# Reordered moves, later bias sums and a copied half row in a deformable convolution kernel

## The chip, the cores and the metric

The kernel runs on one core of a Trainium2 chip. The metric is the device time of one execution in microseconds (us), the median of several runs. The core has five engines with instruction streams of their own: PE (TensorE, matrix products), DVE (VectorE), ACT (ScalarE), POOL (GpSimd) and SP (SyncE, which here issues nearly all DMA transfers). They meet through semaphores; a wait holds everything behind it on its engine.

## The reference

The input x has 8 images of 32 channels and 128 x 128 pixels. Two residual layers follow each other:

```
x1  = x  + conv1(gn(x))          # depthwise 3x3, then three 32x32 channel mixes
out = x1 + conv2(deform(gn(x1)), w_conv) + b_conv

gn(v):      (v - mean) / sqrt(var + 1e-5), per image and channel
deform(v):  off = conv3x3(v, w_off)         # two offsets for each pixel and channel
            at each pixel, v sampled at (row + off[0], col + off[1]),
            clipped to the image, bilinear between the four neighbours
conv2:      3x3, 32 -> 32 channels, zero padding
```

The depthwise convolution and the three mixes are folded into one 3x3 convolution's weights in the setup.

## The kernel before

**Layout.** An image lies in SBUF as 128 partitions: four row phases times 32 channels, with 32 blocks of rows along the free axis. Each 3x3 convolution runs as matmuls over two such tiles, one shifted against the other by two rows: xa and xb for conv1, x1a and x1b for the offsets, mapa and mapb for conv2. The group norm is not applied to the data: its scale goes into the weights (`w1`, `wo`, `w2`, one scaled copy per image, made by DVE), and its mean goes into the padding and into a bias. That bias is a product of the summed weights with the mean: a small matmul (`mean_sum`, L677, "bias sum" below), which ACT then reads from PSUM. There are three of them for each image: b1 (conv1), bo (offsets), b2 (conv2).

**Stages of an image.** conv1 in eight groups of matmuls (jobs "x1"), each evicted by ACT into x1a; then eight offset chunks (L762, 24 matmuls each; counted from 0). Behind each chunk ACT (`offset_parts`), DVE (`deform`) and POOL select and blend neighbours out of x1_strips, which is x1 laid out by strips of rows, and write `mapped`. SP moves `mapped` to mapa in two halves (16 moves each, L456, once four and once eight chunks are mapped) and copies mapa to mapb (L469, L470). Then conv2 runs in eight groups (jobs "c2") and DVE adds them onto x1a, from where SP stores them.

**Order on TensorE.** TensorE runs the chunks of image i; behind each chunk stands a list of jobs (`jobs_behind`): conv1 groups of the next image and conv2 groups of the one before. Image 0's chunks also carry the first three conv1 groups of image 2, with its b1 sum behind chunk 4 (`FURTHER_BIAS`). All jobs share three PSUM banks in turn: a job waits until the third job before it has been evicted (`bank`). A conv1 group 0 waits for `x_pads`, the padding of xa and xb that ACT writes in `pad_x`. The offsets of a chunk wait until the chunk two before it has been used by DVE (`off_used`).

**Order on ACT.** Chunk by chunk, written out by hand (L1017 and on): `offset_parts`, pads of `mapped` at chunks 1 and 5, `pad_x` of the image after next at the chunk `FURTHER_BIAS`, evictions of conv1 groups, `sum_far`, bias evictions, the pads of x1. `clamp` writes the edges of x1_strips after their moves have landed.

**Order on SP.** One stream. For image i: second half of the x1b copy, first mapb copy, the second mapa half and second mapb copy of the image before; loads of the image after next; then x1b's first half and 32 moves x1a to x1_strips for the next image (`move_strips`, L375), and behind these the first mapa half of image i.

**The last image.** Its conv2 reads xa and xb in place of mapa and mapb, in two parts: three groups read the first half of each strip's rows, five the second. The left half of the second part's columns is mapped with the sixth chunk, the right half with the eighth. SP moves the left columns to xa (`move_left_columns`, L479), and copies whole rows from xa to xb (1 MB); ACT, POOL and DVE then copy the right columns out of `mapped` into both tiles (12, 10 and 10 copies, `end_row`). DVE's copies stand behind its third addition of that image (`COPY_END_BEFORE`).

A second path for offsets beyond one pixel stands at the end and isn't taken here.

Of the kernel before, what the change touches and what calls it, by code (L numbers as in the profile page):

```python
# [13 lines left out]
def deformable_preact_kernel(nc, x, dw_w, pw_w, att_w, glob_w, off_w, conv_w, conv_b, out):  # L14
# [8 lines left out]
    Q = C  # L23
# [37 lines left out]
    END_GROUPS = [1, 2, 3, 4, 5, 6, 7, 0]  # L61
    END_PARTS = [0, 0, 0, 1, 1, 1, 1, 1]
    COPY_END_BEFORE = 3
    END_SETUP = 1
    END_BIAS = 5
    CONV2_SETUP = 2
    NEXT_BIAS = [6] * NB
    FURTHER_BIAS = [4] + [NK - 1] * (NB - 1)

    def spread(i):  # L70
        return isinstance(i, int) and NB - 2 <= i < NB
# [20 lines left out]
    def jobs_behind(i, k):  # L92
        jobs = []
        if i + 1 < NB:
            jobs += [("x1", i + 1, m) for m in conv1_groups(i, k)]
            jobs += [("x1", i + 2, m) for m in further_groups(i, k)]
            jobs += [("bo", i + 1, 0)] if k == NEXT_BIAS[i] else []
        if i >= 1:
            jobs += [("b2", i - 1, 0)] if k == (CONV2_SETUP if i + 1 < NB else END_SETUP) else []
            jobs += [("c2", i - 1, m) for m in (LAST_CONV2 if i + 1 < NB else END_CONV2)[k]]  # L100
        if i + 1 == NB and k == END_BIAS:
            jobs += [("b2", i, 0)]
        if i + 2 < NB and k == FURTHER_BIAS[i]:
            jobs += [("b1", i + 2, 0)]
        return jobs

# [10 lines left out]
    with ctx:  # L117
# [6 lines left out]
        def sem(name):  # L124
            return ctx.enter_context(nc.semaphore(name))
# [121 lines left out]
        end_copied = [sem(f"end_rows_copied{n}") for n in range(2)]  # L247
# [81 lines left out]
        def end_row(q, t, o, shifted):  # L329
            p = Q * (2 * t + o)  # L330
            b = NJ * (2 * o + t) + 4
            if not shifted:
                to = xa[Q * q:Q * q + Q, b:b + 4, 1 + WQ:WP]
            elif q < 2:
                to = xb[Q * (q + 2):Q * (q + 3), b:b + 4, 1 + WQ:WP]
            else:
                to = xb[Q * (q - 2):Q * (q - 1), b + 1:b + 5, 1 + WQ:WP]
            return to, mapped[p:p + Q, q, 4:8, 1 + WQ:WP]

        def stored_count(part, images):  # L340

# [79 lines left out]
        def _(sp):  # L421
# [37 lines left out]
            def move_mapa(half):  # L459
                move_rows(mapa, 4 * half, 4, mapa_moved[half])  # L460
# [49 lines left out]
            for i in range(NB):  # L510
                prev, nxt, after = i >= 1, i + 1 < NB, i + 2 < NB
                if prev:

                    sp.wait_ge(off_done, NK * i)
                    copy_x1b(i % 3, 1)
                    sp.wait_ge(map_pads, i)
                    sp.wait_ge(mapa_moved[0], A_MOVES * DMA * i)
                    copy_mapb(0)
                if nxt and i >= 2:
                    sp.wait_ge(out_ready, 8 * (i - 1))  # L520
                    store(sp, i - 2, (i - 2) % 3, 1)
                if prev:
                    sp.wait_ge(mapped_ready, NK * i)
                    if i >= 2:
                        sp.wait_ge(conv2_done, 8 * (i - 1))
                    sp.wait_ge(mapped_pads, 2 * i)
                    move_mapa(1)
                    sp.wait_ge(mapa_moved[1], A_MOVES * DMA * i)
                    copy_mapb(1)
                if after and prev:  # L530
                    for half in range(2):

                        sp.wait_ge(conv1_done, 8 * (i + 1) + (5 if half == 0 else 8))
                        load_xb(i + 2, half, xb_loaded)
                if nxt:

                    sp.wait_ge(x1_pads, i + 2)
                    sp.wait_ge(off_done, NK * i + 4)
                    copy_x1b((i + 1) % 3, 0)
                    sp.wait_ge(mapped_ready, NK * i + 4)  # L540
                    for half in range(2):
                        move_strips(sp, i + 1, half)
                if not nxt:
                    if i >= 2:
                        sp.wait_ge(out_ready, 8 * (i - 1))
# [7 lines left out]
                    copy_rows(xb, xa, 0, 4, end_copied[0])  # L553
                    sp.wait_ge(mapped_pads, 2 * i + 2)
                    sp.wait_ge(mapped_ready, NK * i + 6)
                    move_left_columns(end_moved[1])
                    sp.wait_ge(end_moved[1], A_MOVES * DMA)
                    copy_rows(xb, xa, 4, 4, end_copied[1])
                    sp.wait_ge(out_ready, 8 * i)
                    for part in range(2):  # L560
                        store(sp, i - 1, (i - 1) % 3, part)
                    break
                sp.wait_ge(mapped_ready, NK * i + 4)
                if prev:
                    sp.wait_ge(conv2_done, 8 * (i - 1) + 4)
                else:
                    sp.wait_ge(s_setup["dve"], 6)
                sp.wait_ge(mapped_pads, 2 * i + 1)
                move_mapa(0)
# [52 lines left out]
        def _(pe):  # L622
# [105 lines left out]
            def end_conv2(m, ps):  # L728
                if END_PARTS[m] == 0:
                    pe.wait_ge(end_moved[0], A_MOVES * DMA)  # L730
                    pe.wait_ge(end_copied[0], B_MOVES * DMA)
                else:
                    pe.wait_ge(end_moved[1], A_MOVES * DMA)
                    pe.wait_ge(end_copied[1], B_MOVES * DMA)
                    for e in END_SHARES:
                        pe.wait_ge(end_rows[e], 1)
                conv_group(ps, w2[(NB - 1) % 2], xb, xa, END_GROUPS[m], first2_done, True).then_inc(conv2_done, 1)
# [76 lines left out]
        def _(act):  # L814
# [200 lines left out]
            for i in range(NB):  # L1015
                prev, nxt = i >= 1, i + 1 < NB
                for k in range(NK):  # L1017
# [17 lines left out]
                    if prev and k == (CONV2_SETUP if nxt else END_SETUP):  # L1035
                        conv2_bias(i - 1, (i - 1) % 2, bank("b2", i - 1, 0))
                    if not nxt and k == END_BIAS + 1:
# [8 lines left out]
                    if k == 2:  # L1046
                        if not prev:
                            clamp(i, 1)
                        if not nxt:
                            pad_end(i % 3)  # L1050
                    for m in further_groups(i, k):
                        x1_group(i + 2, i % 2, (i + 2) % 3, m, False, bank("x1", i + 2, m))
                    if nxt and k == NEXT_BIAS[i]:
                        offset_biases(i + 1, (i + 1) % 2, bank("bo", i + 1, 0))
                    if i + 2 < NB and k == FURTHER_BIAS[i]:
                        if k == NK - 1:
                            clamp(i + 1, 0)
                        conv1_bias(i + 2, i % 2, bank("b1", i + 2, 0))
                if nxt and FURTHER_BIAS[i] < NK - 1 or i + 2 == NB:
                    clamp(i + 1, 0)  # L1060
            act.wait_ge(end_copied[1], B_MOVES * DMA)
            act.wait_ge(mapped_ready, NK * NB)
            for which in END_SHARES["act"]:
                to, rows = end_row(*which)
# [38 lines left out]
        def _(pool):  # L1103
# [90 lines left out]

            pool.wait_ge(mapped_ready, NK * NB)
            pool.wait_ge(end_pads, 1)
            pool.wait_ge(end_copied[1], B_MOVES * DMA)
# [20 lines left out]
        def _(dve):  # L1218
# [346 lines left out]
```

## Time and profile before

| what | us |
|---|---|
| median of 3 runs (lowest, highest) | 744.34 (743.94, 746.05) |
| the profiled execution | 743.99 |
| its span in the trace | 742.0 |
| TensorE busy | 688.2 (93%) |
| DVE, POOL, ACT busy | 508.1, 491.5, 459.4 |
| the core's clock, mean granted share | 0.976 |

The trace holds one execution, with times from the span's start. A row of a timeline gives start, length, engine, line of the kernel, operation, what it writes and reads, and in brackets the idle time before it with what ended it. Rows of SPq are issues of DMA transfers; the length is that of the issue, not of the transfer. A matmul in fp32 shows as two instructions; two of 64 columns run beside each other.

### The profile page before, as it was taken

How to read it: one execution, taken by the hardware profiler on the slowest of the kernel's cores; microseconds unless marked ns; L12 is line 12 of the kernel's file. 1: busy time of each engine (PE TensorE's matmuls, PEld its weight loads, DVE VectorE, ACT ScalarE, POOL GpSimd, SP SyncE). 2: the span in 40 equal slices, each digit the busy share in tenths (PEclk: the TensorE clock that was granted, in tenths of full speed). 3: DMA queues.
4: the chain of work that ended last, by engine and by line, in shares of the span. 5: the costliest groups of instructions: out<-in, count | busy, mean ns of one | idle time of the engine just before them, and what ended most of it. 6: DMA issues, size and time to landing. Idle time of an engine off the chain costs nothing.

```text
span 742.0 us, 10713 instructions
## 1 busy us (share of the span) xinstructions
PE 688.2 (93%) x3500; PEld 249.9 (34%) x3500; DVE 508.1 (68%) x1017; ACT 459.4 (62%) x792; POOL 491.5 (66%) x434
## 2 busy tenths in 40 slices
PE   4799979974999999999999999999999999998955
PEld 4233333321333333333333333333333333333312
DVE  3687897574776688567876688567876675756632
ACT  7576767674556765677556765677557755766520
POOL 4014978697367675867867675866867676799920
PEclk9999999996999999999999999999999999999978
DMA  8959706899859896699849995699849444764484
GB/s 142 187 106 154 113 8 144 176 191 167 177 124 222 172 203 146 166 213 205 175 118 230 182 219 127 160 222 199 184 111 220 105 94 114 172 153 112 91 189 99
DMA packets 140732, 116.70 MB, mean 157 GB/s; under 512 B 15200, under 2 KB 114048, under 8 KB 140672
## 3 DMA queue, kind: packets, MB, share of 16 engines
q1 hardware_dynamic: 116640, 104.18, 66.8%
q10 hardware_dynamic: 24032, 11.78, 8.6%
q8 instruction: 29, 0.48, 0.3%
q14 instruction: 31, 0.25, 0.1%
HBM read 31.59 MB, written 16.78 MB: 65 GB/s over the span
## 4 chain that ended last, share of the span: by engine, by line
PE 65%; SPq 8%; POOL 4%; DMA 3%; DVE 3%; ACT 2%; issue 1%; ACTq 0%; POOLq 0%; DVEq 0%
PE off_ps L762 31%; PE c_ps L651 28%; SPq L375 3%; SPq L456 3%; PE c_ps L662 2%; PE c_ps L666 2%; SPq L479 1%; DMA mapa<-mapped 1%; DMA mapb<-mapa 1%; DMA xb<-xa 1%; DVE other_row L1380 1%; POOL other_col L1182 1%; POOL other_col L1179 1%; POOL mapped L1188 1%; POOL other_col L1177 1%
## 5 line engine op out<-in xcount | busy, mean ns | idle before, releaser
L1380 DVE COPY_PREDICATED other_row<-down_ps,row_diff 128x768 f32<-128x768 int32 x128 | 124.8, 1029 | 134.6 <-ACT down_ps L966 134.6
L762 PE MATMUL off_ps<-x1a,wo 128*64 128x512 f32 x768 | 180.0, 602 | 0.4 <-DVE other_row L1392 0.4
L762 PE MATMUL off_ps<-x1b,wo 128*64 128x512 f32 x768 | 177.0, 593 | 0.0
L1176 POOL TENSOR_TENSOR other_row<-other_row,x_strips 128x512 f32<-128x512 f32 x64 | 76.2, 1190 | 152.1 <-DVE other_row L1392 152.1
L651 PE MATMUL c_ps<-xb,w 128*64 128x512 f32 x336 | 152.3, 603 | 9.1 <-ACT xb L1065 9.1
L653 PE MATMUL c_ps<-xa,w 128*64 128x512 f32 x336 | 152.3, 603 | 0.0
L651 PE MATMUL c_ps<-mapb,w 128*64 128x512 f32 x336 | 150.5, 594 | 0.0
L955 ACT ACTIVATE other_row<-row_diff 128x768 f32<-128x768 f32 x128 | 100.8, 836 | 66.9 <-POOL row_diff L1162 43.4
L653 PE MATMUL c_ps<-mapa,w 128*64 128x512 f32 x294 | 131.4, 594 | 0.0
L966 ACT ACTIVATE down_ps<-off_ps,bias_o 128x512 f32<-128x512 f32 x64 | 41.9, 655 | 123.2 <-PE off_ps L762 116.2
L762 PEld LDWEIGHTS off_ps<-x1b,wo 128*64 128x64 f32 x768 | 56.8, 136 | 110.5 <-issue 110.5
L762 PEld LDWEIGHTS off_ps<-x1a,wo 128*64 128x64 f32 x768 | 55.3, 136 | 101.1 <-issue 101.1
L1188 POOL TENSOR_TENSOR mapped<-other_col,other_row 128x512 f32<-128x512 f32 x64 | 81.9, 1279 | 9.5 <-DMA mapa<-mapped 4.6
L1182 POOL TENSOR_TENSOR other_col<-other_col,off_abs 128x512 f32<-128x512 f32 x64 | 82.9, 1295 | 5.0
L1179 POOL TENSOR_TENSOR other_col<-other_col,other_row 128x512 f32<-128x512 f32 x64 | 81.6, 1275 | 5.0
L1177 POOL TENSOR_TENSOR other_col<-other_col,other_row 128x512 f32<-128x512 f32 x64 | 81.6, 1275 | 0.0
L651 PEld LDWEIGHTS c_ps<-xb,w 128*64 128x64 f32 x336 | 45.7, 138 | 104.4 <-issue 104.2
L1160 POOL TENSOR_TENSOR row_diff<-x_strips 128x792 f32<-128x792 f32 x32 | 51.2, 1600 | 37.6 <-ACT x_strips L997 37.6
L651 PEld LDWEIGHTS c_ps<-mapb,w 128*64 128x64 f32 x336 | 44.6, 136 | 89.0 <-issue 89.0
L978 ACT ACTIVATE beyond<-off_abs,minus_one 128x1024 bf16<-128x1024 f32 x64 | 72.9, 1139 | 0.1
L968 ACT ACTIVATE off_abs<-off_ps,bias_o 128x1024 f32<-128x1024 f32 x64 | 70.8, 1106 | 0.0
L1365 DVE SCALAR_TENSOR_TENSOR x1a<-c_ps,bias,x1a 128x512 f32<-128x512 f32 x64 | 45.5, 741 | 19.7 <-PE c_ps L653 19.6
(133 smaller groups left out, 952.4 us busy)
## 6 DMA issues: line engine op xcount, KB each, us to landing
x1b<-x1a SPq DMA_DIRECT2D x28, 520.0 KB, 6.5
mapa<-mapped SPq DMA_DIRECT2D x224, 65.0 KB, 2.1
mapb<-mapa SPq DMA_DIRECT2D x28, 520.0 KB, 6.8
out_dram<-x1a SPq DMA_DIRECT2D x49, 256.0 KB, 4.8
xb<-in_x_dram SPq DMA_DIRECT2D x48, 256.0 KB, 8.6
xa<-in_x_dram ACTq DMA_DIRECT2D x40, 256.0 KB, 7.2
x_strips<-x1a SPq DMA_DIRECT2D x112, 81.2 KB, 2.1
x_strips<-x1a SPq DMA_DIRECT2D x112, 65.0 KB, 2.1
```

The source lines that it names most:

```text
L651: nc.tensor.matmul(bank[0:64, :], weights[:, kx, :], rows_b[:, of, kx:kx + W], start=(kx == 0), stop=(kx == 2))
L653: last = nc.tensor.matmul(bank[64:128, :], weights[:, kx, :], rows_a[:, of, kx:kx + W], start=(kx == 0), stop=(kx == 2))
L762: last = nc.tensor.matmul(off_ps[k % 2][64 * t:64 * t + 64, CH * n:CH * n + CH], wo[wpar][:, kx, side:side + 2 * C], rows[:, b:b + 7:2, kx ...
L955: act.activation(other_row[n][:, :, KR // 2 * odd:KR // 2 * odd + KR // 2, :], diffs_3(row_diff[g // 2 % 2], 2 * (k % 2) + odd), ACT.Copy)
L968: act.activation(off_abs[n][:, :], off_ps[n][:, :], ACT.Abs, bias=bias_o[i % 2][:, 0:1]).then_inc(abs_ready, 1)
L978: act.activation(beyond[:, :], off_abs[k % 2][:, :], ACT.Relu, bias=minus_one[:, :], accum_out=far[i % 2][:, k:k + 1]).then_inc(beyond_rea ...
L1176: step(pool.tensor_tensor(split(column), split(column), own, ALU.add))
L1177: step(pool.tensor_tensor(side, side, other_row[n][:, 0, :, :], ALU.add))
L1179: step(pool.tensor_tensor(side, side, column, ALU.subtract))
L1182: step(pool.tensor_tensor(side, side, off_abs[n][:, 1:2 * CH:2].rearrange("p (h w) -> p h w", h=KR), ALU.mult))
L1188: pool.tensor_tensor(mapped_of_chunk(k), split(side), split(column), ALU.add).then_inc(mapped_ready, 1)
L1380: last = dve.copy_predicated(other_row[n][:, :, KR // 2 * odd:KR // 2 * odd + KR // 2, :], bass.AP(tensor=rows.tensor, offset=rows.offset ...
```

## The change

Four things are changed.

- SP: the 16 moves of image 0's first mapa half go out ahead of image 1's x1b copy and strip moves. Of image 1's 32 strip moves the second 16 go out later, behind the second half of the x1b copy.
- Bias sums on TensorE: b2 goes from chunk 2 to 3 (in the last image from 1 to 2, its own from 5 to 7), image 2's b1 from behind chunk 4 to behind chunk 5. DVE's scaling of the weights stays at its place for b2. ACT's `pad_x` for image 2 follows `FURTHER_BIAS` from chunk 4 to chunk 5.
- Last image: the 1 MB copy of the second part from xa to xb goes. ACT copies the left columns of xb out of `mapped` (16 copies) once six chunks are mapped, behind its own work on all eight.
- The copies of the right columns don't wait for that copy any more, but for the pads.

```diff
-    END_SETUP = 1
-    END_BIAS = 5
-    CONV2_SETUP = 2
+    END_SETUP, END_SETUP_SUM = 1, 2
+    END_BIAS, END_BIAS_SUM = 5, 7
+    CONV2_SETUP, CONV2_SETUP_SUM = 2, 3
-    FURTHER_BIAS = [4] + [NK - 1] * (NB - 1)
+    FURTHER_BIAS = [5] + [NK - 1] * (NB - 1)
...
             jobs += [("x1", i + 1, m) for m in conv1_groups(i, k)]
+            jobs += [("b1", i + 2, 0)] if i == 0 and k == FURTHER_BIAS[i] else []
             jobs += [("x1", i + 2, m) for m in further_groups(i, k)]
...
-            jobs += [("b2", i - 1, 0)] if k == (CONV2_SETUP if i + 1 < NB else END_SETUP) else []
+            jobs += [("b2", i - 1, 0)] if k == (CONV2_SETUP_SUM if i + 1 < NB else END_SETUP_SUM) else []
...
                     copy_x1b(i % 3, 1)
+                    if i == 1:
+                        move_strips(sp, i, 1)
                     sp.wait_ge(map_pads, i)
...
+                if not prev:
+                    sp.wait_ge(mapped_ready, 4)
+                    sp.wait_ge(s_setup["dve"], 6)
+                    sp.wait_ge(mapped_pads, 1)
+                    move_mapa(0)
                 if nxt:
...
-                    for half in range(2):
+                    for half in range(2 if prev else 1):
                         move_strips(sp, i + 1, half)
...
                     move_left_columns(end_moved[1])
-                    sp.wait_ge(end_moved[1], A_MOVES * DMA)
-                    copy_rows(xb, xa, 4, 4, end_copied[1])
...
                     pe.wait_ge(end_moved[1], A_MOVES * DMA)
-                    pe.wait_ge(end_copied[1], B_MOVES * DMA)
+                    pe.wait_ge(end_left, 1)
...
-            act.wait_ge(end_copied[1], B_MOVES * DMA)
+            act.wait_ge(mapped_ready, NK * NB - 2)
+            for q, t, o, shifted in END_ROWS:
+                if shifted:
+                    to, rows = end_row(q, t, o, shifted, slice(0, 1 + WQ))
+                    last = act.activation(to, rows, ACT.Copy)
+            last.then_inc(end_left, 1)
             act.wait_ge(mapped_ready, NK * NB)
...
-                dve.wait_ge(end_copied[1], B_MOVES * DMA)
+                dve.wait_ge(end_pads, 1)
+                dve.wait_ge(mapped_pads, 2 * NB)
                 dve.wait_ge(mapped_ready, NK * NB)
```

## Rows read from the trace of the kernel before

**Rows 1.** Waits of TensorE: line, who ended it, us in total, times, longest

```profile
PE c_ps L662 <- DMA mapb<-mapa: 12.8, 1, 12.8
PE c_ps L651 <- ACT xb L1065: 9.1, 1, 9.1
PE c_ps L677 <- DVE w L1333: 9.0, 2, 5.0
...
PE c_ps L677 <- DVE w L1352: 5.1, 3, 2.4
```

**Rows 2.** Timeline of TensorE, images 0 and 1

```profile
97.73 0.28 PE L677 MATMUL c_ps<-dve_columns,x_strips 128*64 128x1 f32 x4 [3.99 <-DVE w L1333]
...
104.86 0.51 PE L662 MATMUL c_ps<-xb,w 128*32 128x384 f32 x1
...
107.57 2.80 PE L762 MATMUL off_ps<-x1a,wo 128*64 128x512 f32 x12
...
151.57 0.28 PE L677 MATMUL c_ps<-dve_columns,x_strips 128*64 128x1 f32 x4 [2.38 <-DVE w L1352]
...
177.57 0.82 PE L662 MATMUL c_ps<-mapb,w 128*32 128x384 f32 x1 [12.75 <-DMA mapb<-mapa]
```

**Rows 3.** Stretches: length, busy of PE, PEld, DVE, ACT, POOL, granted clock, DMA, GB/s

```profile
97.80:104.90 7.10, 7.10 (x32) 2.51 (x34) 6.36 (x17) 2.46 (x6) 2.59 (x3) 0.76 0.00 0
...
177.60:181.95 4.35, 4.35 (x30) 2.14 (x30) 0.00 (x0) 0.00 (x0) 4.13 (x4) 0.61 1.25 185
```

**Rows 4.** Timeline of SP's issues, images 0 and 1

```profile
110.88 23.91 SPq L375 DMA_DIRECT2D x_strips<-x1a  x32
134.89 10.05 SPq L456 DMA_DIRECT2D mapa<-mapped  x16
...
150.69 12.92 SPq L456 DMA_DIRECT2D mapa<-mapped  x16
```

**Rows 5.** The chain of waits, images 0 and 1: start, us, what

```profile
144.35 2.01 DMA mapa<-mapped
...
162.97 7.06 DMA mapa<-mapped
...
170.74 6.70 DMA mapb<-mapa
...
184.75 5.17 PE off_ps L762 x24
```

**Rows 6.** Timeline of POOL, chunks 3 and 8 (counted from 0)

```profile
96.23 1.27 POOL L1188 TENSOR_TENSOR mapped<-other_col,other_row 128x512 f32<-128x512 f32 x1
...
146.49 1.27 POOL L1188 TENSOR_TENSOR mapped<-other_col,other_row 128x512 f32<-128x512 f32 x1 [4.56 <-DMA mapa<-mapped]
```

**Rows 7.** Timelines of DVE (first row) and ACT around chunk 5

```profile
97.51 1.93 DVE L1380 COPY_PREDICATED other_row<-down_ps,row_diff 128x768 f32<-128x768 int32 x2
...
95.61 0.76 ACT L842 ACTIVATE xb<-dve_columns 128x66 f32<-128x66 f32 x3
...
104.97 0.66 ACT L966 ACTIVATE down_ps<-off_ps,bias_o 128x512 f32<-128x512 f32 x1 [4.71 <-PE off_ps L762]
...
107.28 0.24 ACT L842 ACTIVATE mapped<-dve_columns 128x32 f32<-128x32 f32 x1
```

**Rows 8.** The last image: timelines of five engines, and DVE's line L1449 (min/median/max ns)

```profile
692.13 11.48 SPq L479 DMA_DIRECT2D xa<-mapped  x16
...
712.16 0.42 ACT L1065 ACTIVATE xa<-mapped 32x260 f32<-32x260 f32 x1 [14.55 <-DMA xb<-xa]
...
704.81 1.27 POOL L1188 TENSOR_TENSOR mapped<-other_col,other_row 128x512 f32<-128x512 f32 x1
...
708.62 0.75 DVE L1365 SCALAR_TENSOR_TENSOR x1a<-c_ps,bias,x1a 128x512 f32<-128x512 f32 x1 [1.83 <-PE c_ps L653]
...
L1449 DVE TENSOR_SCALAR xa<-mapped,ones x5: 354/427/432, 712.2 to 715.6; 32x260 f32<-32x260 f32 x5
...
717.69 1.08 PE L651 MATMUL c_ps<-xb,w 128*64 128x512 f32 x1 [9.12 <-ACT xb L1065]
```

More of the change, by code:

```diff
@@ L98, in jobs_behind @@
         if i >= 1:
-            jobs += [("b2", i - 1, 0)] if k == (CONV2_SETUP if i + 1 < NB else END_SETUP) else []
+            jobs += [("b2", i - 1, 0)] if k == (CONV2_SETUP_SUM if i + 1 < NB else END_SETUP_SUM) else []
             jobs += [("c2", i - 1, m) for m in (LAST_CONV2 if i + 1 < NB else END_CONV2)[k]]
-        if i + 1 == NB and k == END_BIAS:
+        if i + 1 == NB and k == END_BIAS_SUM:
             jobs += [("b2", i, 0)]
-        if i + 2 < NB and k == FURTHER_BIAS[i]:
+        if 0 < i < NB - 2 and k == FURTHER_BIAS[i]:
             jobs += [("b1", i + 2, 0)]
@@ L246, in deformable_preact_kernel @@
         end_moved = [sem(f"end_rows_moved{n}") for n in range(2)]
-        end_copied = [sem(f"end_rows_copied{n}") for n in range(2)]
+        end_copied = sem("end_rows_copied")
+        end_left = sem("end_left_columns")
         end_rows = {e: sem(f"end_rows_{e}") for e in ("dve", "act", "pool")}
@@ L327, in deformable_preact_kernel, with end_row @@
         END_SHARES = {"act": END_ROWS[:12], "pool": END_ROWS[12:22], "dve": END_ROWS[22:]}
-        def end_row(q, t, o, shifted):
+        def end_row(q, t, o, shifted, cols=slice(1 + WQ, WP)):
             p = Q * (2 * t + o)
@@ L332, in end_row @@
             if not shifted:
-                to = xa[Q * q:Q * q + Q, b:b + 4, 1 + WQ:WP]
+                to = xa[Q * q:Q * q + Q, b:b + 4, cols]
             elif q < 2:
-                to = xb[Q * (q + 2):Q * (q + 3), b:b + 4, 1 + WQ:WP]
+                to = xb[Q * (q + 2):Q * (q + 3), b:b + 4, cols]
             else:
-                to = xb[Q * (q - 2):Q * (q - 1), b + 1:b + 5, 1 + WQ:WP]
-            return to, mapped[p:p + Q, q, 4:8, 1 + WQ:WP]
+                to = xb[Q * (q - 2):Q * (q - 1), b + 1:b + 5, cols]
+            return to, mapped[p:p + Q, q, 4:8, cols]
         def stored_count(part, images):
@@ L552, in _ @@
                     sp.wait_ge(end_moved[0], A_MOVES * DMA)
-                    copy_rows(xb, xa, 0, 4, end_copied[0])
+                    copy_rows(xb, xa, 0, 4, end_copied)
                     sp.wait_ge(mapped_pads, 2 * i + 2)
@@ L562, in _ @@
                     break
-                sp.wait_ge(mapped_ready, NK * i + 4)
                 if prev:
+                    sp.wait_ge(mapped_ready, NK * i + 4)
                     sp.wait_ge(conv2_done, 8 * (i - 1) + 4)
[L566 to L569, printed above, removed]
+                    sp.wait_ge(mapped_pads, 2 * i + 1)
+                    move_mapa(0)
                 if prev and after:
@@ L730, in end_conv2 @@
                     pe.wait_ge(end_moved[0], A_MOVES * DMA)
-                    pe.wait_ge(end_copied[0], B_MOVES * DMA)
+                    pe.wait_ge(end_copied, B_MOVES * DMA)
                 else:
                     pe.wait_ge(end_moved[1], A_MOVES * DMA)
-                    pe.wait_ge(end_copied[1], B_MOVES * DMA)
+                    pe.wait_ge(end_left, 1)
                     for e in END_SHARES:
@@ L1034, in _ @@
                         x1_group(i + 1, (i + 1) % 2, (i + 1) % 3, m, i + 1 >= 3, bank("x1", i + 1, m))
-                    if prev and k == (CONV2_SETUP if nxt else END_SETUP):
+                    if prev and k == (CONV2_SETUP_SUM if nxt else END_SETUP_SUM):
                         conv2_bias(i - 1, (i - 1) % 2, bank("b2", i - 1, 0))
-                    if not nxt and k == END_BIAS + 1:
+                    if not nxt and k == END_BIAS_SUM:
                         conv2_bias(i, i % 2, bank("b2", i, 0))
@@ L1050, in _ @@
                             pad_end(i % 3)
+                    if i == 0 and k == FURTHER_BIAS[i]:
+                        conv1_bias(i + 2, i % 2, bank("b1", i + 2, 0))
                     for m in further_groups(i, k):
@@ L1057, in _ @@
                             clamp(i + 1, 0)
-                        conv1_bias(i + 2, i % 2, bank("b1", i + 2, 0))
+                        if i > 0:
+                            conv1_bias(i + 2, i % 2, bank("b1", i + 2, 0))
                 if nxt and FURTHER_BIAS[i] < NK - 1 or i + 2 == NB:
                     clamp(i + 1, 0)
-            act.wait_ge(end_copied[1], B_MOVES * DMA)
+            act.wait_ge(mapped_ready, NK * NB - 2)
[4 more added lines that the diff above has]
+            last.then_inc(end_left, 1)
             act.wait_ge(mapped_ready, NK * NB)
@@ L1196, in _ @@
             pool.wait_ge(end_pads, 1)
-            pool.wait_ge(end_copied[1], B_MOVES * DMA)
+            pool.wait_ge(mapped_pads, 2 * NB)
             for which in END_SHARES["pool"]:
```

## The prediction

> **What bounds the kernel now.** I read the waits of TensorE first, because a kernel whose matmuls run nearly without gaps can only be shortened by its gaps, or by work taken off. [rows 1] lists who held TensorE. Four entries matter: 12.8 us for mapb, 9.1 us for a copy on ACT, two waits of 9.0 us together for a weight scaled at L1333, and three of 5.1 us for one scaled at L1352. Of the 9.0 us, 3.99 are image 2's bias sum [rows 2]; the rest is the start of the kernel, which stays. Next I read the timeline of TensorE around each gap, with the granted clock of the stretch behind it: behind the 3.99 us gap it is 0.76 of 2.4 GHz over 7.1 us, behind the 12.8 us gap 0.61 over 4.35 us [rows 3], so a mixture with, and almost wholly at, the 1.2 GHz level. A gap therefore costs its length and some 1.5 to 2 us more. Then came the timelines of the engines that end each gap. Between the 12.8 us gap and the last image TensorE has no gap, so what is gained up to there arrives whole at the last image.
>
> I number the offset chunks through the images: chunk 8 is image 1's first.
>
> **Image 0's moves to mapa.** The 12.75 us gap ends at 177.57 [rows 2]; the chain behind it is one of SP's issues. From 110.88 SP issues 32 strip moves in 23.91 us, then 16 of the first mapa half in 10.05; the second half takes 12.92 from 150.69 [rows 4]. The last of those lands 7.06 us after its issue, and the copy to mapb 6.70 us after its own [rows 5]. Image 0's fourth chunk is mapped at 96.23 + 1.27 = 97.5 [rows 6], and SP is idle then. So the first half can go out from 97.6 to 107.7.
>
> The new order behind it: image 1's first copy to x1b, 0.65 us for each of two issues, to 109.1 (it went out at 109.48, behind the x1 pads, so the 16 moves ahead of it don't make it late; TensorE reads it at 123.2); 16 strips, for which I add 1.2 us to half of 23.91 because the slow first issues (right behind a 1 MB copy) fall into each half: 13.2 us, to 122.3. Image 1's second x1b copy (chunk 7's offsets are done by then) to 123.7, the other 16 strips to 136.9, the first mapb copy to 138.3, the second mapa half, 12.92 us, to 151.3. Its last piece lands 2.0 to 7.1 us later (the two DMA rows of mapa in [rows 5]); I take 2.0, nearest to a stretch without image loads issued just then: 153.3. The copy to mapb adds 0.7 + 6.7: ready at 160.7.
>
> When does TensorE want it? Without the 2.38 us wait before chunk 11 [rows 2] (next edit) it ends chunk 12's offsets at 164.8 - 2.6 = 162.2, where 164.8 is 177.57 - 12.75. The offsets before it must not be late either: chunk 12 needs chunk 10's off_used. ACT and POOL stood before chunk 9 and 8 for the same late mapa moves (POOL 4.56 us [rows 6]); that stall goes, and chunk 10's selection, which ends at 157.6 today, moves ahead by about as much, to 153, before chunk 12's start at 157.0. So conv2 of image 0 starts at 162.2 rather than 177.57: 15.4 us, of which 2.6 are the bias sum. Its first group, 4.35 us at the lower clock [rows 3], takes 2.71 at the full one (104.86 to 107.57 [rows 2]): 1.6 more. Sum up to here **-17.0 us**. Bounds: -18.5 (image 1's own chain of 32 strips, mapa and mapb, which begins with its x1 pads and not with TensorE, comes late next) and -11.7 (mapa landing after 7.1 us: mapb at 165.8, a gap of 3.6, and 1.6 for the clock).
>
> **The strips that stay behind.** Image 1's second half lands at about 139. ACT's clamp, in order on its queue ahead of conv1's evictions, comes to it at about 140.5, so nothing waits; 0, with 1.5 us of room.
>
> **Bias sums a chunk later.** For conv2 (2.38 us in image 1) this is in the sum above. The other two, in image 7, stand beside a loop of ACT, DVE and POOL that sets the pace there: 0. With the sum at chunk 7, c2's last group of image 6 waits for ACT's bias of that chunk, which comes at about 697.9, when TensorE reaches that group today. So the third early group of image 7 still ends near 708.5; gaps of 1.5 us on the way may lower the clock: 0 to +1.7, taken as 0.
>
> Image 2's b1 gives nothing, in my working. The sum moves, but so does ACT's pad_x(2), from chunk 4 to chunk 5, and conv1's first group still follows chunk 5's offsets immediately. TensorE begins these at 97.73 - 3.99 = 93.7, takes 5.2 (24 matmuls, the chain's row in [rows 5]), sums, and stands at 99.1 before x_pads. ACT starts chunk 5's down_ps only when DVE has selected chunk 4's rows, 97.51 + 1.93 = 99.44; from that instruction to the end of pad_mapped it took 107.52 - 104.97 = 2.55 us, and the four fills of pad_x take 1.0 (three of them 0.76) [rows 7]. So x_pads comes at 103.1: a new gap of 4.0 us, as long as the one removed. The group at the lower clock takes 4.35 and ends at 107.45; today it ends at 107.57. **0 us**; -1.8 if the clock does not fall, +1.5 if it stays low into chunk 6.
>
> **xb's left columns.** Today 16 moves from 692.13, their landing, and a copy of 1 MB stand ahead of three engines' copies, which begin at 712.16; TensorE goes on at 717.69 [rows 8]. Now ACT, idle for 14.55 us before that, makes 16 copies of 0.43 us (6.9) from about 697.9, done at 704.8. The moves to xa land by 705. Chunk 63 is mapped at 704.81 + 1.27 = 706.1: ACT's 12 copies end at 711.3, POOL's 10 earlier. DVE must first add the third group, 708.62 + 0.75 = 709.4, and its ten copies at a pitch of 0.43 (eight pitches between 712.2 and 715.6) end at 713.7. That is late next; TensorE starts 0.3 later, at 714.0: **-3.7 us**. Bounds: -5.5 (DVE's copies hardly longer than ACT's end) and -1.5 (the clock cost above).
>
> In [rows 8] DVE's shortest of these copies is 0.354 us and the others 0.42 to 0.43, beside POOL's. The Trainium skill (SBUF — State Buffer, Who interferes with whom) says that DVE's copies in a two-port mode and GpSimd's instructions exclude each other for a whole instruction. By that, DVE's last six copies, for which POOL is done, would be shorter than 0.43, and the end some 0.5 us or more better.
>
> **Sum.** -17.0 + 0 - 3.7 = -20.7. The profiled execution took 743.99 us (span 742.0 and 2.0 around it), 0.35 under the median of the runs: 723.3 in its terms, and 723.6 beside the median of 744.34. I predict **723.6**.
>
> **Rivals.**
> 1. mapb stays late in image 0. For it: the slack is 1.5 us (160.7 against 162.2), and ACT's loads of image 3 lie in the same stretch, as in the 7.06 us landing. Against it: those loads go out near 133 and 158, not beside the mapa moves' tail. Gap and clock give 5.2 back: about 729. The Trainium skill (DMA: Bandwidth & Descriptors, Issuing engines are not separate DMA queues) says that transfers issued by different engines run on the same DMA engines and interleave; it speaks for this rival, and the 7.06 beside 2.01 agrees.
> 2. image 2's b1 does gain: the gap before x_pads is short, or the clock holds. Then 721 to 722. Against it: ACT's order.
> 3. DVE's last six copies run at the 0.354 us of its shortest, POOL being done, or less: 0.5 to 1.2 us, so 722.4 to 723.1.
> 4. The end gives little, since TensorE runs at 1.2 GHz after its gaps before the third early group: 725.5 to 727.
> 5. Slower: image 1's second strips, now behind the x1b copy, hold ACT's clamp, and with it evictions, selection and the offsets that TensorE needs. Each us beyond 140.5 holds ACT, each beyond about 144 TensorE too (chunk 12's offsets have 4 us of room). To eat 20.7 us the strips would have to land after 165, where I have 139: above 744.7. Nothing in the trace delays 16 small moves by 25 us.
> 6. The moves don't come earlier, because SP is held by another wait in front of them (the setup's reads of mapa, the pads of mapped): then only the 3.7 of the end and no more than that is left, 740 to 744. Against it: image 0's mapping and ACT's pads are done at 97.5, and SP has nothing else to do.
>
> **How the numbers follow.** Forecast 0.56 (721.5 to 726), rival 1 0.16, rival 2 0.08, rival 3 0.07, rival 4 0.09, rival 5 0.02, rival 6 0.02. The range 719.0 to 729.5 takes in the bounds -18.5 - 5.5 = -24 (720.3) with 1.3 more for b1, and rival 1; it leaves under 2 in 10 outside. What can be told from no change is 0.3%, 2.2 us: faster 0.96, within 0.02, slower 0.02.
>
> **What would show it.** In the timeline of SP, mapa from 97.6 and the second mapa half from about 138. In TensorE's waits: no mapb wait (or under 2 us), no L1352 wait in image 1, and a new wait of about 4 us for ACT's fill of xb (L842) in place of the one for L1333. At the end, a wait of about 5.5 us for DVE's copies rather than 9.1 for ACT's. The prediction is wrong if the x_pads wait is absent, if mapb still holds TensorE by more than 3 us, or if a wait appears between 185 and 636.

## The result and the profile after

| | before | after |
|---|---|---|
| median of 13 runs each, us | 744.24 | 734.42 |
| the profiled execution, us | 743.99 | 733.47 |
| its span, us | 742.0 | 731.7 |
| mean granted clock | 0.976 | 0.986 |

The ratio is 0.9882, with a 95% interval of 0.9856 to 0.9907; it is reckoned from the single runs without one of 747.89 us, in which the granted clock was lower (0.941), and so isn't the quotient of the two medians. The change gains 9.8 us; the prediction had 20.7, and 734.42 lies above its range (719.0 to 729.5). Line numbers of the kernel after are higher: by 2 on SP's lines, by 5 on TensorE's and on most of ACT's (off_ps is L767), by 13 or 14 on DVE's, POOL's and on ACT's copies at the end (L1449 is L1463).

TensorE's waits after, as in [rows 1] (line, who ended it, us in total, times, longest):

```profile
PE c_ps L667 <- DMA mapb<-mapa: 7.9, 2, 7.0
...
PE c_ps L656 <- DVE xb L1463: 4.9, 1, 4.9
PE c_ps L682 <- DVE w L1346: 4.7, 1, 4.7
PE c_ps L667 <- ACT xb L847: 4.1, 1, 4.1
```

The wait for mapb is still there, 7.9 us in place of 12.8. Its place tells more than its size. TensorE's timeline after, images 0 to 2 and the end:

```profile
103.77 0.48 PE L667 MATMUL c_ps<-xb,w 128*32 128x384 f32 x1 [4.08 <-ACT xb L847]
...
163.72 0.48 PE L667 MATMUL c_ps<-mapb,w 128*32 128x384 f32 x1 [0.90 <-DMA mapb<-mapa]
...
169.06 2.75 PE L767 MATMUL off_ps<-x1a,wo 128*64 128x512 f32 x12
...
220.02 0.64 PE L656 MATMUL c_ps<-xb,w 128*64 128x512 f32 x1 [1.27 <-ACT x1a L919]
...
255.73 0.82 PE L667 MATMUL c_ps<-mapb,w 128*32 128x384 f32 x1 [7.00 <-DMA mapb<-mapa]
...
263.73 2.75 PE L767 MATMUL off_ps<-x1a,wo 128*64 128x512 f32 x12
...
607.82 2.76 PE L767 MATMUL off_ps<-x1a,wo 128*64 128x512 f32 x12
...
708.99 1.09 PE L656 MATMUL c_ps<-xb,w 128*64 128x512 f32 x1 [4.93 <-DVE xb L1463]
```

and the same chunks before, where conv2 of image 1 began without a wait:

```profile
184.58 2.75 PE L762 MATMUL off_ps<-x1a,wo 128*64 128x512 f32 x12
...
262.69 0.51 PE L662 MATMUL c_ps<-mapb,w 128*32 128x384 f32 x1
...
268.03 2.75 PE L762 MATMUL off_ps<-x1a,wo 128*64 128x512 f32 x12
...
612.14 2.75 PE L762 MATMUL off_ps<-x1a,wo 128*64 128x512 f32 x12
```

TensorE's lead over the kernel before, at the same chunk, is a ledger of the change. Chunk 13: 184.58 - 169.06 = 15.5 us. The chunk behind conv2 of image 1: 268.03 - 263.73 = 4.3. Image 6: 612.14 - 607.82 = 4.3. Behind the end's wait: 717.69 [rows 8] - 708.99 = 8.7; the span: 10.3. So image 0 gave 15.5 us of the 17.0 forecast, the end gave 6.0 rather than 3.7, and 11.2 us were **given back in image 1**: 7.0 of wait, 2.7 because the stretch behind it took 263.73 - 255.73 = 8.0 us rather than 5.3, and 1.3 in the wait at 220.02. (Ahead of that short wait ACT had stood 10.87 us for a store that SP issues.) The granted clock shows the 2.7: the first stretch runs at full clock behind the 0.90 us wait, the second near the 1.2 GHz level (columns as in [rows 3]).

```profile
163.72:168.00 4.28, 4.28 (x38) 2.23 (x40) 3.72 (x15) 4.19 (x6) 4.12 (x4) 1.00 1.26 184
255.73:261.60 5.87, 5.87 (x34) 2.89 (x36) 1.99 (x5) 0.51 (x1) 3.86 (x4) 0.53 1.25 199
```

Why is mapb of image 1 late? SP's timeline after, as in [rows 4]:

```profile
98.29 10.62 SPq L458 DMA_DIRECT2D mapa<-mapped  x16
...
140.69 13.45 SPq L458 DMA_DIRECT2D mapa<-mapped  x16
155.56 0.65 SPq L471 DMA_DIRECT2D mapb<-mapa  x1
156.25 0.64 SPq L472 DMA_DIRECT2D mapb<-mapa  x1
156.93 16.46 SPq L440 DMA_DIRECT2D xb<-in_x_dram  x8
173.49 2.08 SPq L450 DMA_DIRECT2D x1b<-x1a  x1
175.62 0.61 SPq L451 DMA_DIRECT2D x1b<-x1a  x1
176.27 24.48 SPq L377 DMA_DIRECT2D x_strips<-x1a  x32
...
229.70 12.69 SPq L458 DMA_DIRECT2D mapa<-mapped  x16
243.81 0.65 SPq L471 DMA_DIRECT2D mapb<-mapa  x1
244.50 0.64 SPq L472 DMA_DIRECT2D mapb<-mapa  x1
```

From 98 to 245 us no gap between two issues is longer than 1.5 us, so SP itself sets the pace. Its copy goes out at 244.50, only 6.8 us earlier than before (251.31), while TensorE is ready for it at 248.73, 14.0 us earlier (262.69). The 8 loads of xb take 16.46 us to issue (9.78 before, from 171.42), and everything behind them is later by as much. ACT's loads of the next images' xa meet SP's transfers; its own queue, after:

```profile
157.78 1.30 ACTq L365 DMA_DIRECT2D xa<-in_x_dram  x2
...
243.56 0.32 ACTq L365 DMA_DIRECT2D xa<-in_x_dram  x1
243.92 1.04 ACTq L365 DMA_DIRECT2D xa<-in_x_dram  x2
244.99 0.94 ACTq L365 DMA_DIRECT2D xa<-in_x_dram  x1
```

Each load is four issues of 256 KB, 1 MB together. They start within 2.3 us of SP's mapb copies, in image 0 and in image 1. The second copy goes out at 244.50 and TensorE starts at 255.73: 11.2 us later, where [rows 5] had 6.70. The DMA views of the two copies, first after from 243 to 256 us, then before from 250 to 262 (q1 is SP's queue and q10 ACT's: packets, MB, share; then issues, KB, median us to landing):

```profile
q1 hardware_dynamic: 1029, 1.35, 54.6%
q10 hardware_dynamic: 2087, 1.04, 44.1%
...
mapb<-mapa SPq DMA_DIRECT2D x2, 520.0 KB, 9.6
```

```profile
q1 hardware_dynamic: 2472, 2.03, 90.0%
q10 hardware_dynamic: 50, 0.03, 1.4%
...
mapb<-mapa SPq DMA_DIRECT2D x2, 520.0 KB, 5.8
```

With ACT's queue taking 44.1% the copy needs 9.6 us, with 1.4% it needs 5.8. The Trainium skill (DMA: Bandwidth & Descriptors, Issuing engines are not separate DMA queues) says that transfers of all issuing engines interleave on the same DMA engines; these rows agree.

So the theory (**A**): the change removed a gap that had given SP and ACT room. Now TensorE and ACT are 15 us earlier, SP is not as much earlier, and ACT's loads, which follow conv1, fall beside SP's copies. The rivals: SP's lateness alone is the cause, or the collision alone, or another part of the change costs what image 0 gained.

### The profile page after: what moved, and what is told of

Its sections match the earlier page's. It is cut to its first block, busy times and chain, and to the rows that moved or that the text cites. A ratio compares the mean times of both kernels' runs of the same rounds, so it can differ in the third digit from the quotient of the medians.

```text
span 731.7 us, 10726 instructions
## 1 busy us (share of the span) xinstructions
PE 687.3 (94%) x3500; PEld 246.1 (34%) x3500; DVE 508.1 (69%) x1017; ACT 465.0 (64%) x808; POOL 491.2 (67%) x434
## 4 chain that ended last, share of the span: by engine, by line
PE 55%; SPq 5%; POOL 5%; DVE 4%; DMA 2%; issue 1%; ACT 1%; POOLq 0%; DVEq 0%; ACTq 0%
PE off_ps L767 25%; PE c_ps L656 25%; SPq L458 3%; PE c_ps L667 2%; PE c_ps L671 2%; DMA mapb<-mapa 2%; DVE other_row L1393 1%; SPq L409 1%; POOL other_col L1195 1%; POOL other_col L1192 1%; POOL mapped L1201 1%; POOL other_col L1190 1%; POOL other_row L1189 1%; POOL row_diff L1173 1%; PE c_ps L675 1%
## 5 line engine op out<-in xcount | busy, mean ns | idle before, releaser
L767 PE MATMUL off_ps<-x1a,wo 128*64 128x512 f32 x768 | 176.8, 594 | 1.1 <-DVE other_row L1405 1.1
L767 PE MATMUL off_ps<-x1b,wo 128*64 128x512 f32 x768 | 176.2, 592 | 0.0
L767 PEld LDWEIGHTS off_ps<-x1b,wo 128*64 128x64 f32 x768 | 55.0, 135 | 110.3 <-issue 110.3
L767 PEld LDWEIGHTS off_ps<-x1a,wo 128*64 128x64 f32 x768 | 53.8, 135 | 103.6 <-issue 101.6
L1350 DVE BATCH_NORM_STATS2 stats<-x1a 128x6 f32<-128x512 f32 x64 | 42.3, 685 | 26.6 <-ACT x1a L919 26.5
```

Of the source, the lines that this page charges most:

```text
L767: last = nc.tensor.matmul(off_ps[k % 2][64 * t:64 * t + 64, CH * n:CH * n + CH], wo[wpar][:, kx, side:side + 2 * C], rows[:, b:b + 7:2, kx ...
```

## The experiments

The kernel before stood beside all of them (medians 743.67 to 744.06). Ratios are to it.

**The parts alone.** Only the new order of SP:

```
+                    if i == 1:
+                        move_strips(sp, i, 1)
...
+                if not prev:
+                    sp.wait_ge(mapped_ready, 4)
+                    sp.wait_ge(s_setup["dve"], 6)
+                    sp.wait_ge(mapped_pads, 1)
+                    move_mapa(0)
...
-                    for half in range(2):
+                    for half in range(2 if prev else 1):
```

> The kernel before with the move of image 0's moves to mapa (and of image 1's second strips) alone. Theory A: from image 0 to image 1's conv2 the bound is SP's stream of moves with the transfers it issues, which in the changed kernel runs without a break from 98 to 245 us; TensorE, now ahead of it, waits for mapb in image 1 (7.0 us, and 2.6 more at the lower clock). By A image 1's conv2 begins at 255 to 257 here too, though TensorE keeps the 2.4 us wait for its bias sum in image 1: the wait for mapb there is 5 to 7 us, and the time is 5 to 7 us under before, 737.5 to 739.5. Rival B: the removed waits simply add up, and image 1's gap comes from the moved bias sums: then no gap at image 1's conv2, and 13 to 15 us under before, 729 to 731.

Measured: 740.22 us, 0.9957 [0.9932, 0.9982]. Conv2 of image 0 starts at 165.65 with 1.91 us of wait, the b2 wait of image 1 is gone by itself, and conv2 of image 1 waits 7.76 us for mapb. The time lies 0.7 us above theory A's range and 9 above B's: A's wait is there, a little longer than I expected. Only the end (ACT's copies of the left columns in place of SP's copy):

> The kernel before with the end alone: xb's left columns copied by ACT, no 1 MB copy. Both theories: the wait of TensorE between the two parts of the last conv2 falls from 9.1 to about 5 us, ended by DVE's copies; 3.5 to 6 us under before, 738 to 740.7. A rival (the end's gain comes only together with the later bias sum, whose 2.0 us wait and lower clock lay in the same image): under 2 us.

Measured: 738.79 us, 0.9936 [0.9913, 0.9959]: 4.9 us from the end alone, with the 12.45 us mapb wait in its old place. The two alone gain 3.5 and 4.9, together 8.3; the whole change has 9.8. So no other part costs 11 us: what is lost is lost with SP's moves alone too.

**b1 back behind chunk 4**, all else as after:

```
-    FURTHER_BIAS = [5] + [NK - 1] * (NB - 1)
+    FURTHER_BIAS = [4] + [NK - 1] * (NB - 1)
```

> The changed kernel with image 2's bias sum and its padding back at chunk 4. My step said that this part gives nothing: the 4.1 us wait for ACT's padding is replaced by the old 4.0 us wait for the weights, image 0's conv2 begins within 1 us of 163.7 and image 1's within 1.5 us of 255.7; time within 2 us of the changed kernel's 734.4. Rival: the later bias sum was worth its 4 us (or costs them): 4 us or more away.

Measured: 736.44 us, 0.9907 [0.9879, 0.9935], which can't be told from the change's 0.9882. TensorE's timeline shows the old wait back, as long as the new one was:

```profile
97.72 0.28 PE L682 MATMUL c_ps<-dve_columns,x_strips 128*64 128x1 f32 x4 [4.06 <-DVE w L1346]
```

The trace of this run comes from an execution of 740.78 us, 4.3 over the median. In it conv2 of image 1 begins at 253.29 behind 3.89 us of wait, 2.4 us before the changed kernel's (I had expected 1.5 at most), and a wait of 6.16 us for mapb stands ahead of conv2 of image 3:

```profile
253.29 0.82 PE L667 MATMUL c_ps<-mapb,w 128*32 128x384 f32 x1 [3.89 <-DMA mapb<-mapa]
...
429.27 0.82 PE L667 MATMUL c_ps<-mapb,w 128*32 128x384 f32 x1 [6.16 <-DMA mapb<-mapa]
```

SP's copy of image 1 goes out as in the changed kernel (244.54 beside 244.50), but ACT's loads go out 0.7 us later or more (the first at 244.23), and the two copies land after 6.9 us (median) rather than 9.6. So small a shift between two queues goes with a shorter wait in image 1, and with a new one in image 3, where the runs that relieve SP (below) have one too.

**pad_x(2) a chunk earlier**, all else as after:

```
-                    if i + 2 < NB and k == FURTHER_BIAS[i]:
+                    if i + 2 < NB and k == (FURTHER_BIAS[i] if i else 4):
                         pad_x(i + 2, i % 2)
```

> The changed kernel with ACT's padding for image 2 at chunk 4 as before, the bias sum staying behind chunk 5: TensorE loses the 4.1 us wait for the padding and the lower clock behind it, 4 to 6 us, in image 0. Theory A: SP's stream doesn't move, so the wait for mapb in image 0 grows from 0.9 to 4 to 7 us, image 1's conv2 still begins at 254 to 257, and the time is within 2 us of 734.4. Rival B (TensorE's gaps add up): image 1's conv2 begins 4 to 6 us earlier, and the time is 728.5 to 730.5.

Measured: 735.2 us, 0.9864 [0.9832, 0.9897]. The x_pads wait went, but not into mapb of image 0, as I had expected: TensorE now waits for DVE's selection.

```profile
103.46 2.80 PE L767 MATMUL off_ps<-x1a,wo 128*64 128x512 f32 x12 [0.59 <-DVE other_row L1405]
...
114.81 4.49 PE L767 MATMUL off_ps<-x1a,wo 128*64 128x512 f32 x12 [3.33 <-DVE other_row L1405]
```

In this stretch DVE holds TensorE: from 95 to 120 us it is busy for 23.2 of 25 us (TensorE 21.1, ACT 17.9, POOL 17.3). In these two runs a bias sum or a pad moved about changed which instruction waits, and not the time. Conv2 of image 1 begins at 257.80, again behind 7.66 us of wait for mapb.

**ACT's second xa load one chunk later**, for all images from 3 on:

```
-                        if prev and i + 2 < NB and 4 * half + 3 in groups:
+                        if prev and i + 2 < NB and 4 * half + 3 in (
+                                groups if half == 0 else conv1_groups(i, k - 1) if k else []):
```

> The changed kernel with ACT's second x load of an image (xa, half 1, for image 3 and later) issued one chunk later, so that in image 1 it no longer starts with the mapb copy. Theory A (SP, which issues without a break from 98 to 245 us, gets its mapb copy out late, and ACT's xa loads then make the copy's landing 11.1 us instead of 6.7): the copy is issued as before at 244.5 and lands some 6.7 us later, near 251.3; TensorE's wait ahead of conv2 of image 1 falls from 7.0 to about 2.6 us, and the low-clock group behind it from 5.9 to about 5; the time falls by 4 to 6 us against the changed kernel, to 728 to 731. Theory B (the copy is slow for another reason, such as SP's own xb loads issued right behind it): the landing stays near 11 us, the wait near 7 us, and the time stays at 733 to 736.

Measured: 729.58 us, 0.9795 [0.9744, 0.9846]. No wait of a microsecond for mapb is left in any image; xb's issues take 9.77 us, and SP is 6 us earlier in image 1. That I had not expected: theory A left the copy where it was and let only its landing shorten, so this run mixes the two causes, and the runs with one load late below take them apart. In place of it stands one wait of 3.40 us at 199.81 for DVE: its statistics of image 3 stand in order behind the later load ([4.62 <-DMA xa<-in_x_dram] at 186.39). The executions of this kernel spread from 723.80 to 740.04 us.

**SP relieved in two ways.** Image 1's 16 second strips issued in SP's idle time ahead of image 0's mapa moves (in the form of image 0's strips, without the border columns):

```
-                if i > 0:
+                if i > 0 and not (i == 1 and half == 1):
...
-                    if i == 1:
-                        move_strips(sp, i, 1)
...
                 if not prev:
+                    sp.wait_ge(strips_loaded[1], strips_count(1, 0))
+                    for strip in range(4):
+                        sp.wait_ge(x1_ready, 8 + min(2 * strip + 3, 8))
+                        move_strip(sp, 1, 1, strip)
                     sp.wait_ge(mapped_ready, 4)
```

> The changed kernel with image 1's 16 strips of half 1 issued ahead of image 0's mapa moves, where SP is idle, rather than at 125 us: 14.1 us of issues leave SP's unbroken stretch. Theory A (SP's stretch is what is late in image 1): mapa (half 0) of image 0 goes out 10 to 14 us earlier than 140.7 or at the moment when its rows are there, image 1's second mapa moves start when ACT's fill of mapped's border is done (226.1 us in the changed kernel, against 229.7), so the mapb copy goes out some 3.6 us earlier, and TensorE's wait ahead of conv2 of image 1 falls from 7.0 to 1 to 3.5 us; time 726 to 731. Theory B (ACT's loads alone are the cause): the copy goes out up to 3.6 us earlier but lands with the loads no more than 1 us earlier; wait 6 to 7, time 733 to 735. Theory C (the early strips themselves push mapa's moves of image 0 back): SP's stretch from 125 us on starts no earlier and the time is 734 or more.

and image 3's xb loads cut short:

```
-                    sp.dma_start(to[Q * q:Q * q + Q, first:first + HB, 1:W + 1], rows[:, b:e, (q + 2) % 4, :])\
+                    n = 2 if isinstance(i, int) and i == 3 else HB
+                    sp.dma_start(to[Q * q:Q * q + Q, first:first + n, 1:W + 1], rows[:, b:b + n, (q + 2) % 4, :])\
```

> The changed kernel that loads only the first two blocks of rows of each half of image 3's xb, in the same 8 issues (the rest of xb keeps the image before, so image 3 is computed from wrong data). Theory A (these 8 issues, 16.5 us from 156.9 instead of the 9.8 that the trace of before showed, hold back x1b and the strips of image 2): the issues take about 5 to 7 us, x1b of image 2 goes out when its borders are filled, near 170.2 instead of 173.5, and SP reaches image 1's second mapa moves near ACT's fill of the border at 226.1; the wait ahead of conv2 of image 1 falls from 7.0 to 1 to 3.5 us, the time to 726 to 731. Theory B (SP's start in image 1 does not matter, ACT's loads beside the copy do): x1b goes out earlier but the wait stays at 6 to 7 us and the time at 733 to 735.

Measured: 734.29 us, 0.9869 [0.9833, 0.9906], and 735.47 us, 0.9873 [0.9839, 0.9906]: no better than the change. Yet theory A's steps came true in image 1: x1b went out at 169.26 and 170.24 (173.49 after), the copy at 237.76 and 239.16 (244.50), and conv2 of image 1 did not wait; with xb cut short it begins at 247.56, where the changed kernel begins at 255.73:

```profile
247.56 0.51 PE L668 MATMUL c_ps<-mapb,w 128*32 128x384 f32 x1
```

The wait came back two images later, in the kernel with early strips as

```profile
420.58 0.82 PE L669 MATMUL c_ps<-mapb,w 128*32 128x384 f32 x1 [7.02 <-DMA mapb<-mapa]
```

where SP's copy and ACT's load again go out together, first SP's queue, then ACT's:

```profile
408.65 0.65 SPq L471 DMA_DIRECT2D mapb<-mapa  x1
409.35 0.64 SPq L472 DMA_DIRECT2D mapb<-mapa  x1
...
408.42 0.86 ACTq L365 DMA_DIRECT2D xa<-in_x_dram  x2
```

The copies land after 9.3 us there (median), with ACT's queue at 48.1% of the engines' time. With xb cut the wait is 7.97 us in the same image; ACT's load (411.86) goes out beside the last mapa moves, and the copy (416.46) follows. So SP's lateness alone is not the cause: SP made earlier moves the wait to another image. That the meeting makes the wait of image 3 is read off these rows; the next run, with late loads, is without it. My forecast of 726 to 731 for both was wrong there, because I looked at image 1 alone once more.

**Both edits together** (early strips, late loads):

> Both edits together: the strips ahead of image 0's mapa moves and ACT's second xa load one chunk later. Theory A: the mapb copy goes out near 240 us and lands near 247, before TensorE needs it (248.7), so the wait ahead of conv2 of image 1 is 0 to 0.5 us and the low clock behind it is gone; 7.0 plus about 1.5 us less than the changed kernel: 725 to 727.5. Theory B: what the two edits save is the same microseconds, and something else in image 1 (an x1 strip, the selection on VectorE) holds TensorE for 4 us or more in their place: 729 or more.

Measured: 726.99 us, 0.9774 [0.9737, 0.9811], faster than the change and the lowest median of all, though its interval overlaps those of the other runs with late loads. The waits for mapb are 0.7 us (image 1) and 0.8 (at 638.18). One new wait of 2.95 us is left, again through DVE's statistics behind a late load:

```profile
282.55 0.72 PE L658 MATMUL c_ps<-mapb,w 128*64 128x512 f32 x1 [2.95 <-DVE x1a L1381]
```

**One load at a time.** Only image 3's load late (it meets SP's xb loads in image 0), with `groups if half == 0 or i != 1 else ...`:

> The changed kernel with only image 3's second xa load issued one chunk later (the load that in the changed kernel goes out at 157.8 us, beside SP's xb loads). Theory A (the collision of ACT's second xa load with the mapb copy is what costs, in whatever image it falls, and SP's start only moves it): xb's 8 issues take near 10 us instead of 16.5, x1b of image 2 goes out near 171, the copy of image 1 near 238 us, and conv2 of image 1 waits 0 to 1 us; but the copy of a later image meets the loads, with a wait of 5 to 8 us in image 2 or 3, as where the strips went early or xb was cut: 731 to 736. Theory B (this one collision, in image 0, makes SP late for good, and nothing else is wrong): no wait for mapb in any image, and the time is that with all loads late, 728 to 731.

and only image 4's (it meets image 1's mapb copy), with `i != 2`:

> The changed kernel with only image 4's second xa load issued one chunk later (the load that goes out at 243.6 us, beside the mapb copy of image 1). Theory A: SP's stretch is as in the changed kernel (xb 16.5 us, x1b of image 2 at 173.5, copy at 244.5), but the copy lands 6 to 7.5 us after its issue instead of 11.1, so the wait ahead of conv2 of image 1 falls from 7.0 to 2.5 to 3.5 us, 4 us less than the changed kernel: 729 to 731.5, if no copy of a later image meets a load; 733 to 736 if one does. Theory B (only the collision in image 0 matters): the wait stays at 6 to 7 us and the time at 733 to 736.

Measured: 730.35 us, 0.979 [0.9728, 0.9851], and 728.89 us, 0.9797 [0.9752, 0.9842]. With image 4's load alone out of the way everything on SP stays as it was, xb's 16.19 us and the copy at 245.22 included; only the landing changes. TensorE's wait, and the granted clock behind it:

```profile
251.99 0.48 PE L667 MATMUL c_ps<-mapb,w 128*32 128x384 f32 x1 [3.31 <-DMA mapb<-mapa]
```

```profile
251.99:256.27 4.28, 4.28 (x38) 2.23 (x40) 4.28 (x6) 3.77 (x8) 1.61 (x2) 1.00 1.24 194
```

7.00 became 3.31, and the clock stays full: 3.7 of wait and the 2.7 behind it, against 5.5 between the medians. This is the clean separation: the meeting of one 1 MB load with one copy is worth about half of what image 1 took back. The remaining 3.3 us are SP's lateness: with xb cut short above, the copy went out 5.3 us earlier and no wait was left. Image 3's load is what makes SP late: with this load out of the way, xb takes 9.76 us and the copy goes out at 238.82. Conv2 of image 1 does not wait there, but this run can't show that the earlier copy does it, because TensorE is itself later: a wait for DVE of 5.09 us came at 202.68, behind image 3's late load (7.44 us in front of its statistics), and conv2 of image 1 begins at 254.00. I had expected a wait for mapb in a later image; none came. The executions of this run spread from 723.16 to 733.21 us.

**A control: the same late loads in the kernel before.**

> The kernel before, with nothing of the change, and ACT's second xa load one chunk later for image 3 and later. A control: if the 4.8 us that this edit saves in the changed kernel come from a collision that the change brought about, it saves nothing here, because the mapb copies of the kernel before (170.7 and 251.3 us) do not have these loads (160.5 and 257.7 us) beside them, and the 12.5 us wait ahead of conv2 of image 0 stays: 742 to 746. If the edit is a gain of its own, the time falls by 4 us or more, to 740 or less.

Measured: 744.25 us, 0.9995 [0.9967, 1.0024]. The time is that of the control, but not for the reason I gave. The gap of image 0 did shrink, and another wait took its place:

```profile
172.55 0.82 PE L662 MATMUL c_ps<-mapb,w 128*32 128x384 f32 x1 [7.78 <-DMA mapb<-mapa]
...
296.79 0.97 PE L651 MATMUL c_ps<-mapb,w 128*64 128x512 f32 x1 [4.36 <-DVE x1a L1366]
```

The mapa moves, issued until 163.43, are followed by the copy at 164.84; in the kernel before, the last landed 7.06 us after its issue [rows 5], with ACT's loads out at 160.51; here they go out at 170.47. So the collision was in the trace before, in image 0, and the 7.06 was its mark: the change did not bring such meetings about. In the changed kernel they fall on xb's issues in image 0 and on the copy in image 1. In the kernel before the late edit is no gain of its own, because the wait for DVE takes back what it saves.

**Late loads only from image 5 on, with early strips:**

```
-                                groups if half == 0 else conv1_groups(i, k - 1) if k else []):
+                                groups if half == 0 or i < 3 else conv1_groups(i, k - 1) if k else []):
```

> The changed kernel with image 1's strips of half 1 ahead of image 0's mapa moves, and ACT's second xa load one chunk later from image 5 on (not for images 3 and 4). Theory A: no wait for mapb in image 1 (as with the early strips alone), none of 5 us or more in images 2 and 3, because the loads no longer meet the copies there, and the 2.95 us wait of image 2 for VectorE (put down to image 4's late load, for which its statistics waited 6.1 us) is gone: 723.5 to 726.5. Theory B: where image 4's load is not late, its meeting the copy of image 1 delays SP by 5 to 6 us once more, and a wait of 4 us or more for mapb comes back in image 2 or 3: 729 to 735.

Measured: 732.33 us, 0.9848 [0.9822, 0.9874]. The 2.95 us wait and the long mapb waits are gone, as theory A has it, but in the trace (an execution of 737.83 us, 5.5 over the median) two longer waits for DVE came, for statistics 7.6 and 8.6 us behind late loads:

```profile
370.01 1.11 PE L658 MATMUL c_ps<-mapb,w 128*64 128x512 f32 x1 [4.48 <-DVE x1a L1381]
...
544.92 1.11 PE L658 MATMUL c_ps<-mapb,w 128*64 128x512 f32 x1 [5.44 <-DVE x1a L1381]
```

Why images 5 and 7 pay for a late load here, and not in the version with both edits, where the same loads are late, is open, and so is whether the other executions had these waits. A load a whole chunk later has little room of its own in front of DVE.

## Why the prediction was wrong

- **Image 0's moves, -17.0: right up to image 0, wrong as a gain of the kernel.** Conv2 of image 0 starts at 163.72 rather than 162.2, at full clock, and the lead is 15.5 us. The step that failed is the sentence "Between the 12.8 us gap and the last image TensorE has no gap, so what is gained up to there arrives whole at the last image". No gap before meant only that the slack there was smaller than 15 us, and I had not worked it out. The bound named the next chain, "image 1's own chain of 32 strips, mapa and mapb", but let it begin to matter only at -18.5, 1.5 us past this step's gain, and shows no working for that. Measured, the chain that was late runs from xb's issues (16.5 us, where they took 9.8 before) through image 2's strips and image 1's mapa to a copy that TensorE could read 11.2 us after its issue, and 11.2 us of the 15.5 go back.
- **Rival 1 had the mechanism and the wrong place.** It asked whether ACT's loads make mapb late in image 0, where the wait is 0.90 us. It is xb's issues in image 0 and the next image's copy that they meet. The 7.06 us of [rows 5] was the mark: I used it as the other end of a bound, not as a fact about who else was loading.
- **Strips, 0: right for TensorE, wrong for ACT.** The prediction has the strips landed at about 139 and "nothing waits". ACT's clamp waits 3.52 us for them, until 144.50; no wait of TensorE appears behind it before 163.72.

```profile
144.50 0.31 ACT L990 ACTIVATE x_strips<-x_strips 32x128 f32<-32x128 f32 x1 [3.52 <-DMA x_strips<-x1a]
```

- **Bias sums, 0: right,** with the new x_pads wait of 4.08 us at 103.77 where I had 4.0; putting the sum back brings the old wait of 4.06. Moving b2 was not needed in image 1: with SP's moves alone that wait went too.
- **The end, -3.7: right in its wait, too small as a sum.** TensorE's wait is 4.93 us (I had 5.5), and the lead grows by 4.4 there. Behind the wait it grows by another 1.6, for which the sum had no term: in the 4.31 us behind it the granted clock is 0.68, where it was 0.50 before. That makes 6.0, past the bound of 5.5; alone the edit gave 4.9. The shorter wait is rival 3: seven copies take 0.34 to 0.35 us rather than 0.43. DVE's copies after, beside POOL's until 706.15 and then without them (ACT's go on until 706.95):

```profile
705.88 0.42 DVE L1463 TENSOR_SCALAR xa<-mapped,ones 32x260 f32<-32x260 f32 x1
706.32 0.34 DVE L1463 TENSOR_SCALAR xb<-mapped,ones 32x260 f32<-32x260 f32 x1
706.68 0.35 DVE L1463 TENSOR_SCALAR xa<-mapped,ones 32x260 f32<-32x260 f32 x1
```

- The prediction named its own failure: "or if a wait appears between 185 and 636". It did, at 255.73. In sum: 20.7 forecast, less 1.5 in image 0 and 11.2 in image 1, and 2.3 more at the end, make the 10.3 us of the span.

## What to carry to other kernels

A stage without a gap has slack of unknown size. Before an earlier start is carried to the end of the kernel, rebuild the next stage's chain on every queue at the shifted times, and see which transfers of other queues then meet its copies. A DMA that took three times as long as its like (7.06 against 2.01 us) marks such a meeting. And a relief that only shifts a queue in time has to be followed through all images: twice here it moved the same wait from image 1 to image 3. The trace of one execution shows where the waits fell in that execution only.

## What was not expected of the hardware

- The issues themselves stretch beside another queue's transfers: the same 8 loads of xb take 9.8 us of SP's time alone, and 16.5 us beside ACT's 1 MB load; everything in order behind them pays. Busy DMA engines are not enough for that: their busy share (as in [rows 3]) is 1.10 while the issues take 9.8 us, before the change, and 1.16 while they take 16.5.
- The granted clock behind a short wait is not a matter of the wait's length alone. Behind 3.31 us (late load of image 4) it stayed at 1.00 over the next 4.28 us; behind 3.33 us (padding a chunk earlier, at 114.81) it was 0.62 over the next 4.49, and behind 2.95 us (both edits, at 282.55) 0.57 over the next 3.95. So the prediction's 1.5 to 2 us for the clock behind a gap is no constant: behind 7.00 us it was 2.7, behind 3.31 nothing. What else decides is open.
